# Attention values with P as the moving operand: one matmul per head for four half products

## The chip, the cores and the metric

One core of a Trainium2 chip runs the whole program. The metric is the device time of one execution in microseconds (us). The kernel before took 1598.1 us as the median of 3 runs (1597.1 to 1598.14).

## The reference

Two layers with residuals on x of shape (32, 128, 1024), all in float32. The first mixes the 128 rows of each batch by a matrix gathered with that batch's index; the second is causal attention with 16 heads of 64 columns.

```python
w = weights[conditions]                       # 200 matrices of 128x128
x = x + einsum('bct,bcd->bdt', x, w)
q, k, v = (heads(einsum('bsd,ed->bse', x, W)) for W in (Wq, Wk, Wv))
q = q * minimum(cond, 4.0)
scores = einsum('bhqd,bhkd->bhqk', q, k) / sqrt(64)
attn = softmax(where(causal, scores, min), axis=-1)
out = einsum('bhqk,bhkd->bhqd', attn, v)
x = x + einsum('bsd,ed->bse', rejoined(out), Wo)
```

## The kernel before

The stages are: an opening (first layer for batch 0, lines 384 to 394, and the first blocks of V from line 646); the rest of the first layer with V for the other batches; the attention stage, from step T_ATT to T_END; the output products of four batches; and fourteen pairs of batches of output products at the end. V, the halves of X, attention rows and prepared weights go through scratch in HBM.

The attention stage has 16 groups (8 groups of four batches, twice for half of the heads) of four cells, 64 cells. A cell n is one pair of heads for four batches and has 16 steps: eight for the q block, eight for the k block, both in TensorE's banks PJ. The scores, masks, exponentials, norms, turns and values of the cell are placed in the steps of the next one, at a step a that lies five after its k block:

- `pe_scores` (line 726): per batch one product of 256 columns, the two heads beside each other; the other head's rows of K are zero.
- DVE masks and takes the row maximum (lines 1126, 1132), ACT exponentiates with the row sum (957), DVE takes the reciprocal (1136), POOL multiplies (1239). P stands in PP with queries in the partitions.
- `dve_turn` (line 1011): ten transposes of 32 partitions per cell, five at a + 8 and five at a + 13, put the blocks on and below the diagonal at their turned place in PT.
- ACT makes PTH from PT (line 962, at a + 14), POOL makes PTL (1243).
- `pe_values` (line 737): per batch three matmuls of 256 columns, at a + 18 and a + 20; V's chunk of 128 columns (both heads) is stationary and the turned P of both heads moves. Half of what comes out pairs a head with the other head's P and is dropped.
- ACT copies the rows that are used to AT (lines 970, 971), and SP stores them (1538).

V of a group comes in two transfers (line 1400); ACT and POOL split it (921, 1233) into VH and VL. X of the next group comes in eight pieces, six steps apart (line 1388). Beside this, in a step of 48 of the cells that is otherwise quiet, a piece of Wq, Wk (16 of them) or Wo (32) is split by ACT and DVE (934 and 1107, 986 and 1150) and stored. Wq and Wk of the second half of the heads are loaded during the eighth and ninth group (line 1364), and Wo from 34 steps ahead of T_END.

Of the kernel before, what the change touches and what calls it, by code (L numbers as in the profile page):

```python
# [45 lines left out]
def cond_attention(nc, x, idx, cond, w0, wq, wk, wv, wo, mask_d, ident_d, out):  # L46
# [14 lines left out]
    with ExitStack() as ctx:  # L61
# [46 lines left out]
        with nc.sbuf_tensor("t_Y1", [128, DC, 256], f32) as tile:  # L108
            Y1 = tile
        VH = [sb("VH0", [128, GB, 512], f32r)]  # L110
# [7 lines left out]
        with ExitStack() as early:  # L118
            BH = sb("BH", [128, 4, 512], f32r, early)
            BL = sb("BL", [128, 4, 512], f32r, early)  # L120
        VH.append(sb("VH1", [128, GB, 512], f32r))
# [23 lines left out]
        WEH = sb("WEH", [128, 4, 512], f32r)  # L145
        WEL = sb("WEL", [128, 4, 512], f32r)
# [9 lines left out]
        QL = sb("QL", [128, T], f32r)  # L156
        PTH = sb("PTH", [128, GB, 256], f32r)
        PTL = sb("PTL", [128, GB, 256], f32r)
        AT = sb("AT", [128, 2, 2, 2, 128])
# [7 lines left out]
        PV = [pb("PV0"), pb("PV1")]  # L167
# [23 lines left out]
        act_pt, pool_pt, act_at = sem("pt_high"), sem("pt_low"), sem("at_out")  # L191
# [9 lines left out]
        l_y = [sem(f"load_y{n}") for n in range(2)]  # L201
# [4 lines left out]
        s_at = [[sem(f"store_at{n}_{k}") for k in range(2)] for n in range(2)]  # L206
# [13 lines left out]
        mask_at, exp_at, recip_at, norm_at, turn0_at, turn1_at, half_at, ptl_at, at_at = (At() for _ in range(9))  # L220
# [124 lines left out]
        for j in range(NGRP):  # L345
            t0 = T_ATT + STEPS * j
            for c in range(NC):
# [1254 lines left out]
```

## Time and profile before

| | us |
|---|---|
| median of 3 runs | 1598.1 |
| profiled execution | 1599.05 |
| its span, first to last instruction | 1597.7 |
| TensorE busy | 1587.2 (99%) |
| VectorE busy | 1016.6 (64%) |
| ScalarE busy | 820.4 (51%) |
| GpSimd busy | 739.2 (46%) |

The profile is of one execution; its own time is the span and 1.35 us around it. PE is TensorE's matmuls and PEld its weight loads, which overlap them. Busy times of one engine's groups overlap as well where its instructions are pipelined, so the distance from one matmul's start to the next one's says more than its duration.

### The profile page before, as it was taken

The numbers are of one execution on the slowest core, as the hardware profiler recorded it, in microseconds if no ns is written. First come the engines' busy times: TensorE is split into PE (matmuls) and PEld (weight loads), VectorE is DVE, ScalarE is ACT, GpSimd is POOL, SyncE is SP. The second block draws the span as 40 slices with busy tenths as digits, with TensorE's granted clock in tenths as the row PEclk, the third lists the DMA queues.
The fourth block names the chain that finished last, engine by engine and source line by source line (L and its number), as shares of the span: only waits on it lengthen the run. The fifth ranks groups of instructions, "written<-read, shape, count | busy, mean of one in ns | idle before, by whom it ended". The sixth has DMA issues, their size and how long they took to land.

```text
span 1597.7 us, 23102 instructions
## 1 busy us (share of the span) xinstructions
PE 1587.2 (99%) x7810; PEld 1338.5 (84%) x7810; DVE 1016.6 (64%) x2008; ACT 820.4 (51%) x2221; POOL 739.2 (46%) x618
## 2 busy tenths in 40 slices
PE   8999999999999999999999999999999999999999
PEld 7888888888888888888888888888888888888887
DVE  5844544543577777777776777777777755555553
ACT  6645545542466666665666666566666632222220
POOL 1545555552344434434544553454455334555552
PEclk9999999999999999999999999999999999999999
DMA  9857888866954465455529654553542596444442
GB/s 325 326 219 273 311 289 283 291 235 211 315 179 160 146 206 169 165 139 177 164 85 299 197 153 139 176 152 132 161 158 80 204 333 254 174 168 165 165 158 86
DMA packets 162086, 320.43 MB, mean 201 GB/s; under 512 B 13746, under 2 KB 81586, under 8 KB 155826
## 3 DMA queue, kind: packets, MB, share of 16 engines
q1 hardware_dynamic: 161970, 318.97, 59.1%
q8 instruction: 62, 1.02, 0.3%
q14 instruction: 54, 0.44, 0.1%
HBM read 184.70 MB, written 134.22 MB: 200 GB/s over the span
## 4 chain that ended last, share of the span: by engine, by line
PE 93%; DVE 2%; SPq 2%; DMA 1%; POOL 0%; issue 0%; ACT 0%; ACTq 0%; POOLq 0%
PE p_PJ L642 21%; PE p_PJ L643 21%; PE p_PJ L644 20%; PE p_SC L644 6%; PE p_SC L643 6%; PE p_SC L642 6%; PE p_PV L642 3%; PE p_PV L644 3%; PE p_PV L643 3%; PE p_LP L642 1%; PE p_LP L644 1%; PE p_LP L643 1%; SPq L1364 1%; PE p_PV L774 1%; PE p_LP L774 1%; DVE t_WSL L1103 1%
## 5 line engine op out<-in xcount | busy, mean ns | idle before, releaser
L643 PE MATMUL p_PJ<-t_XL,t_WH 128*128 128x512 f32 x1008 | 394.7, 392 | 0.0
L642 PE MATMUL p_PJ<-t_XH,t_WH 128*128 128x512 f32 x1008 | 394.6, 391 | 0.0
L644 PE MATMUL p_PJ<-t_XH,t_WL 128*128 128x512 f32 x1008 | 392.1, 389 | 0.0
L1243 POOL TENSOR_TENSOR t_PTL<-t_PT,t_PTH 128x512 fp32r<-128x512 f32 x128 | 163.0, 1294 | 382.5 <-ACT t_PTH L962 382.5
L1021 DVE STREAM_TRANSPOSE t_PT<-t_PP 32x256 f32<-32x256 f32 x640 | 278.2, 435 | 10.9 <-POOL t_PP L1239 1.2
L957 ACT ACTIVATE t_PP<-t_PP,t_st 128x128 f32<-128x128 f32 x512 | 198.5, 390 | 50.1 <-DVE t_st L1132 50.0
L644 PEld LDWEIGHTS p_PJ<-t_XH,t_WL 128*128 128x128 f32 x1008 | 189.3, 188 | 40.6
L642 PEld LDWEIGHTS p_PJ<-t_XH,t_WH 128*128 128x128 f32 x1008 | 189.8, 188 | 31.1
L643 PEld LDWEIGHTS p_PJ<-t_XL,t_WH 128*128 128x128 f32 x1008 | 190.2, 189 | 29.9
L962 ACT ACTIVATE t_PTH<-t_PT 128x512 fp32r<-128x512 f32 x128 | 73.8, 624 | 194.7 <-DVE t_PT L1021 194.7
L1239 POOL TENSOR_TENSOR t_PP<-t_PP,t_st 128x512 f32<-128x512 f32 x128 | 132.7, 1043 | 55.0 <-DVE t_st L1136 55.0
L1126 DVE SCALAR_TENSOR_TENSOR t_PP<-p_SC,t_beta,t_mask 128x256 f32<-128x256 f32 x256 | 111.5, 477 | 45.1 <-PE p_SC L644 45.1
L1113 DVE TENSOR_TENSOR t_KL<-p_PJ,t_KH 64x512 fp32r<-64x512 f32 x128 | 88.2, 689 | 53.4 <-ACT t_KH L944 51.3
L1233 POOL TENSOR_TENSOR t_VL<-t_VX,t_VH 128x512 fp32r<-128x512 f32 x64 | 92.0, 1458 | 65.0 <-ACT t_VH L921 65.0
L944 ACT ACTIVATE t_KH<-p_PJ 64x512 fp32r<-64x512 f32 x128 | 75.8, 592 | 87.2 <-PE p_PJ L644 85.6
L1228 POOL TENSOR_TENSOR t_xl<-t_XT,t_xh 128x512 fp32r<-128x512 f32 x56 | 74.4, 1328 | 95.0 <-ACT t_xh L844 94.3
L957 ACT ACTIVATION_READ_ACCUMULATOR t_PP<-t_PP,t_st 128x1 f32 x512 | 95.9, 187 | 0.0
L1132 DVE TENSOR_REDUCE t_st<-t_PP 128x2 f32<-128x256 f32 x256 | 94.1, 409 | 0.0
L1136 DVE RECIPROCAL t_st<-t_st 128x4 f32<-128x4 f32 x128 | 22.8, 178 | 87.2 <-ACT t_PP L957 87.2
L1087 DVE TENSOR_TENSOR t_SL<-t_SUM,t_SH 128x512 fp32r<-128x512 f32 x42 | 32.4, 772 | 69.6 <-ACT t_SH L875 69.6
L642 PE MATMUL p_PV<-t_PTH,t_VH 128*128 128x256 f32 x256 | 72.0, 281 | 1.6 <-POOL t_PTL L1243 1.6
L644 PE MATMUL p_PV<-t_PTH,t_VL 128*128 128x256 f32 x256 | 72.3, 282 | 0.0
(248 smaller groups left out, 3602.9 us busy)
## 6 DMA issues: line engine op xcount, KB each, us to landing
t_XH<-xth_scratch SPq DMA_DIRECT2D x56, 512.0 KB, 6.4
t_XL<-xtl_scratch SPq DMA_DIRECT2D x56, 512.0 KB, 6.6
v_scratch<-t_VR SPq DMA_DIRECT2D x64, 256.0 KB, 4.2
xth_scratch<-t_XH SPq DMA_DIRECT2D x16, 1024.0 KB, 3.9
xtl_scratch<-t_XL SPq DMA_DIRECT2D x16, 1024.0 KB, 6.3
t_VX<-v_scratch SPq DMA_DIRECT2D x32, 512.0 KB, 4.9
at_scratch<-t_AT SPq DMA_DIRECT2D x128, 128.0 KB, 1.8
t_XT<-x SPq DMA_DIRECT2D x31, 512.0 KB, 4.7
```

Of the source, the lines that this page charges most:

```text
L642: pe.matmul(bank, lh, rh, start=first, stop=False, skip_group_check=goes_on)
L643: pe.matmul(bank, lh, rl, start=False, stop=False, skip_group_check=goes_on)
L644: return pe.matmul(bank, ll, rh, start=False, stop=last, skip_group_check=goes_on)
L944: act.activation(KH[r, :, 128 * h:128 * h + 128], pj[r], ACT.Copy).then_inc(act_k, 1)
L957: act.activation(PP[:, u, h, :], PP[:, u, h, :], ACT.Exp, bias=st[:, 0, u, h:h + 1], scale=1.0, accum_out=st[:, 1, u, h:h + 1]).then_inc(a ...
L1021: m = dve.transpose(pt[32 * j:32 * j + 32, :, 32 * i:32 * i + 32], pp[32 * i:32 * i + 32, :, 32 * j:32 * j + 32])
L1113: dve.tensor_tensor(KL[r, :, k], pj[r], KH[r, :, k].bitcast(f32), ALU.subtract).then_inc(dve_k, 1)
L1126: dve.scalar_tensor_tensor(out=PP[:, u], in0=SC[u // 2][:, 256 * (u % 2):256 * (u % 2) + 256].rearrange("p (h k) -> p h k", h=2), scalar=b ...
L1132: dve.tensor_reduce(st[:, 0, u, :], PP[:, u], AX, ALU.max, negate=True).then_inc(dve_m, 1)
L1233: pool.tensor_tensor(VL[j % 2][:, u, :], VX[:, u, :], VH[j % 2][:, u, :].bitcast(f32), ALU.subtract).then_inc(pool_vl, 1)
L1239: pool.tensor_tensor(pp, pp, r, ALU.mult).then_inc(pool_n, 1)
L1243: pool.tensor_tensor(PTL[:, u:u + 2], PT[:, u:u + 2], PTH[:, u:u + 2].bitcast(f32), ALU.subtract).then_inc(pool_pt, 1)
```

## The change

Values. V is stored as VV, per batch and head a block of 128 columns that holds the high and the low half of that head's 64 columns side by side (for the second head of a pair in the other order). P is stored as PS, per batch and head 256 columns, the high half and then the low half. One matmul per head has the first as its stationary and the second as its moving operand. It gives four products in one bank half: V high x P high and V high x P low in 64 partitions, V low x P high and V low x P low in the other 64.

```diff
-            to = PV[k][:, z * 256:z * 256 + 256]
-            three(to, VH[j % 2][:, u, cc], VL[j % 2][:, u, cc], PTH[:, u, :], PTL[:, u, :], True, True).then_inc(pe_pv, 1)
+            for h in range(2):
+                moving = PS[:, 2 * u + h].rearrange("p a q -> p (a q)")
+                mm = pe.matmul(PV2[:, z, 256 * h:256 * h + 256], VV[j % 2][:, u, 2 * c + h, :], moving, start=True, stop=True)
+            mm.then_inc(pe_pv, 1)
```

Both banks now hold one pair of batches, and the values of a pair wait until DVE has summed the pair before (`dve_M`). ACT copies V low x P high across to the partitions that it belongs to (AC), DVE adds the two products of V high in PSUM by a reduction, and POOL adds the two.

```diff
-                    act.activation(dst[0:64], pv[0:64, :, 0, :], ACT.Copy).then_inc(act_at, 1)
-                    act.activation(dst[64:128], pv[64:128, :, 1, :], ACT.Copy).then_inc(act_at, 1)
+                    act.activation(AC[0:64, k], PV2[64:128, :, 0:128], ACT.Copy).then_inc(act_c, 1)
+                    act.activation(AC[64:128, k], PV2[0:64, :, 256:384], ACT.Copy).then_inc(act_c, 1)
...
+                    for h in range(2):
+                        r = slice(64 * h, 64 * h + 64)
+                        both = PV2[r, :, 256 * h:256 * h + 256].rearrange("p u (a q) -> p u q a", a=2)
+                        dve.tensor_reduce(AT[r, k], both, AX, ALU.add).then_inc(dve_M, 1)
...
+                    pool.tensor_tensor(AT[:, P % 2], AT[:, P % 2], AC[:, P % 2], ALU.add).then_inc(pool_at, 1)
```

Turning. DVE transposes 32x32 blocks of all 128 partitions at once, two batches per instruction, into TB; ten transfers of 32 partitions with 1 KB each take the blocks on and below the diagonal to their rows, in one of two tiles by turns. The turn of the next cell waits for these transfers, and so does ACT's high half of P, which stands in ACT's order ahead of the high half of K.

```diff
-            for i, j in tri[5 * part:5 * part + 5]:
-                m = dve.transpose(pt[32 * j:32 * j + 32, :, 32 * i:32 * i + 32], pp[32 * i:32 * i + 32, :, 32 * j:32 * j + 32])
+            pp = PP[:, 2 * k:2 * k + 2].rearrange("p u h (j c) -> p j (u h) c", j=4)
+            dve.transpose(turned(n)[:, :, 4 * k:4 * k + 4, :], pp).then_inc(dve_t, 1)
...
+            for i in range(4):
+                for j in range(i + 1):
+                    src = turned(n)[32 * i:32 * i + 32, j].rearrange("a u q -> a (u q)")
+                    sp.dma_start(p_tile(n)[32 * j:32 * j + 32, i, :], src).then_inc(l_P, 16)
```

The order of a cell, of the loads of X and of the loads of V:

```diff
-                turn0_at.put(a + 8, n)
-                turn1_at.put(a + 13, n)
+                move_at.put(a + 10, n)
...
-                    half_at.put(a + 14 + k, P)
-                    ptl_at.put(a + 15 + 2 * k, P)
-                    v = a + 17 + k if n == 4 * NGRP - 1 else a + 18 + 2 * k
+                    turn_at.put(a + 7.5 + 1.5 * k, P)
+                    last = n == 4 * NGRP - 1
+                    half_at.put(a + (20 if last else 25.25) + 0.5 * k, P)
+                    ptl_at.put(a + (20.75 if last else 26) + 1.5 * k, P)
+                    v = a + (25.25 + 3.25 * k if last else 29 + 4.5 * k)
+                    own = v + (1.75 if n >= 4 * NGRP - 2 else (1.75, 8.5)[k])
...
-                    at_at.put(v + (0.75 if n == 4 * NGRP - 1 else 5.25), P)
+                    other_at.put(v + 0.75, P)
+                    own_at.put(own, P)
+                    at_at.put(own + 1.25, P)
...
-                    X_load.put(t0 - STEPS + (12 + 5 * i if j == 1 else 24 + 4 * i if j == NG + 1 else 1 + 6 * i), (j, i))
+                    X_load.put(t0 - STEPS + (12 + 5 * i if j == 1 else 24 + 4 * i if j == NG + 1 else (1, 6, 17, 22, 33, 38, 49, 54)[i]), (j, i))
...
-                V_load.put(t0 + (-11, 2.75)[k] if j == 0 else t0 - STEPS + (28 if j == 1 else 0.25), (j, k))
+                V_load.put(t0 + (-11, 2.75)[k] if j == 0 else t0 - STEPS + (28 if j == 1 else 10), (j, k))
```

Opening. ACT's fourth weight copy and the second batch's weight copy come later, and TensorE gets nine matmuls of zeros.

```diff
-            w_high.put((-8.5, -7.75, -6, -5, -0.5, 0.5, 1.5, 2.5)[d], d)
-            w_low.put((-7.5, -6.5, -5, -4, 0.5, 1.5, 2.5, 3.5)[d], d)
+            w_high.put((-8.5, -7.75, -6, -2.75, -0.5, 0.5, 1.5, 2.5)[d], d)
+            w_low.put((-7.5, -6.5, -5, -2, 0.5, 1.5, 2.5, 3.5)[d], d)
...
-            l0_wh.put(p - 1, bb)
-            l0_wl.put(p - 0.5, bb)
+            l0_wh.put(p - (0.5 if bb == 1 else 1), bb)
+            l0_wl.put(p - (0.25 if bb == 1 else 0.5), bb)
...
                     pe_l0_a(bb, h)
+                    if bb == 0 and h == 1:
+                        pe_zeros(3)
...
                     pe_l0_b(bb, h)
+                    if bb == 0 and h == 1:
+                        pe_zeros(6)
```

For room, the rows of the output stage use one buffer where they had two, and some tiles of the last cells lie elsewhere.

## Rows read from the trace of the kernel before

**Rows 1.** The page: busy us per engine; the chain that ended last, by engine

```profile
PE 1587.2 (99%) x7810; PEld 1338.5 (84%) x7810; DVE 1016.6 (64%) x2008; ACT 820.4 (51%) x2221; POOL 739.2 (46%) x618
...
PE 93%; DVE 2%; SPq 2%; DMA 1%; POOL 0%; issue 0%; ACT 0%; ACTq 0%; POOLq 0%
```

**Rows 2.** Busy us by stretch, granted clock, DMA share, GB/s

```profile
0.00:20.00 20.00, 15.53 (x62) 11.91 (x63) 10.55 (x19) 12.85 (x23) 3.11 (x10) 1.00 0.84 298
...
480.00:900.00 420.00, 418.91 (x2189) 359.67 (x2188) 314.77 (x726) 261.92 (x819) 194.30 (x160) 1.00 0.55 173
```

**Rows 3.** Waits of PE from 450 to 1360 us: total, times, longest

```profile
PE p_PV L642 <- POOL t_PTL L1243: 1.6, 2, 1.1
```

**Rows 4.** Groups of PE: shapes and count, busy us, mean ns, idle before

```profile
L643 PE MATMUL p_PV<-t_PTL,t_VH 128*128 128x256 f32 x256 | 72.2, 282 | 0.0
```

**Rows 5.** Timeline of PE and its weight loads, one cell: start, us

```profile
701.36 0.28 PE L642 MATMUL p_SC<-t_KH,t_QH 128*128 128x256 f32 x1
...
704.18 0.28 PE L642 MATMUL p_PV<-t_PTH,t_VH 128*128 128x256 f32 x1
704.18 0.19 PEld L643 LDWEIGHTS p_PV<-t_PTL,t_VH 128*128 128x128 f32 x1
...
704.89 0.40 PE L642 MATMUL p_PJ<-t_XH,t_WH 128*128 128x512 f32 x1
...
715.18 0.28 PE L642 MATMUL p_SC<-t_KH,t_QH 128*128 128x256 f32 x1
```

**Rows 6.** Groups of DVE, ACT and POOL from 480 to 1360 us

```profile
L1021 DVE STREAM_TRANSPOSE t_PT<-t_PP 32x256 f32<-32x256 f32 x592 | 257.4, 435 | 10.3 <-POOL t_PP L1239 1.2
...
L1132 DVE TENSOR_REDUCE t_st<-t_PP 128x2 f32<-128x256 f32 x236 | 86.7, 409 | 0.0
...
L971 ACT ACTIVATE t_AT<-p_PV 64x256 f32<-64x256 f32 x120 | 45.5, 379 | 2.9
...
L1243 POOL TENSOR_TENSOR t_PTL<-t_PT,t_PTH 128x512 fp32r<-128x512 f32 x120 | 152.8, 1294 | 362.5 <-ACT t_PTH L962 362.5
```

**Rows 7.** Timeline of DVE in the same cell

```profile
707.43 0.69 DVE L1116 TENSOR_TENSOR t_QL<-p_PJ,t_QH 128x512 fp32r<-128x512 f32 x1 [0.45 <-ACT t_QH L952]
...
710.38 1.07 DVE L1150 TENSOR_TENSOR t_OL<-t_xr,t_OH 128x512 fp32r<-128x512 f32 x1
711.92 1.41 DVE L1113 TENSOR_TENSOR t_KL<-p_PJ,t_KH 64x512 fp32r<-64x512 f32 x2 [0.48 <-ACT t_KH L944]
```

**Rows 8.** Timeline of ACT and POOL in the same cell

```profile
706.59 0.19 ACT L957 ACTIVATION_READ_ACCUMULATOR t_PP<-t_PP,t_st 128x1 f32 x1
706.80 0.60 ACT L952 ACTIVATE t_QH<-p_PJ 128x512 fp32r<-128x512 f32 x1
...
707.07 1.04 POOL L1239 TENSOR_TENSOR t_PP<-t_PP,t_st 128x512 f32<-128x512 f32 x1 [0.50 <-DVE t_st L1136]
```

**Rows 9.** Timeline of SP's queue: stores of attention rows

```profile
721.91 1.13 SPq L1538 DMA_DIRECT2D at_scratch<-t_AT  x2
```

**Rows 10.** The view of line 1538, the stores of attention rows

```profile
DMA to landing us min/median/max: 1.7/1.8/10.9
```

**Rows 11.** The view of line 1364, the loads of Wq and Wk

```profile
DMA to landing us min/median/max: 4.4/8.1/13.1
```

**Rows 12.** The page's DMA issues: KB each, median us to landing

```profile
t_XH<-xth_scratch SPq DMA_DIRECT2D x56, 512.0 KB, 6.4
```

**Rows 13.** Timeline of PE and ACT in the opening

```profile
11.03 0.66 PE L774 MATMUL p_LP<-t_ident,t_XT 128*128 128x128 f32 x4 [0.53 <-ACT t_XT L900]
11.53 0.65 PE L774 MATMUL p_PV<-t_ident,t_XT 128*128 128x128 f32 x4
13.79 0.47 PE L642 MATMUL p_PJ<-t_WSH,t_XH 128*128 128x512 f32 x1 [1.61 <-DVE t_XL L1035]
...
12.13 0.31 ACT L895 ACTIVATE t_wh<-t_wr 128x128 fp32r<-128x128 f32 x1 [0.66 <-POOL t_wr L1220]
12.34 0.58 ACT L856 ACTIVATE t_XH<-p_LP 128x512 fp32r<-128x512 f32 x1
```

More of the change, by code:

```diff
@@ L109, in cond_attention @@
             Y1 = tile
+        with nc.sbuf_tensor("t_VV0", [128, GB, 8, 128], f32r) as tile:
+            VV = [tile]
         VH = [sb("VH0", [128, GB, 512], f32r)]
@@ L120, in cond_attention @@
             BL = sb("BL", [128, 4, 512], f32r, early)
+        with nc.sbuf_tensor("t_VV1", [128, GB, 8, 128], f32r) as tile:
+            VV.append(tile)
         VH.append(sb("VH1", [128, GB, 512], f32r))
@@ L145, in cond_attention @@
         WEH = sb("WEH", [128, 4, 512], f32r)
+        with nc.sbuf_tensor("t_TB", [128, 4, 8, 32], f32) as tile:
+            TB = tile
+            with nc.sbuf_tensor("t_PT2", [128, GB, 256], f32) as tile:
+                PT2 = tile
         WEL = sb("WEL", [128, 4, 512], f32r)
@@ L200, in cond_attention @@
         l_V = [sem(f"load_v{n}") for n in range(2)]
-        l_y = [sem(f"load_y{n}") for n in range(2)]
+        l_y = sem("load_y")
         l_x1 = [sem(f"load_x1_{n}") for n in range(4)]
@@ L205, in cond_attention @@
         s_V = [sem(f"store_v{n}") for n in range(4)]
-        s_at = [[sem(f"store_at{n}_{k}") for k in range(2)] for n in range(2)]
+        s_at = [sem(f"store_at{k}") for k in range(2)]
         s_out = [sem(f"store_out{n}") for n in range(4)]
@@ L566, in operand, with turned, p_tile, v_high @@
             return tuple(four(h) for h in halves)
+        def turned(n):
+            return TB[:] if n < 58 else WR[:].rearrange("p a (b c) -> p (a b) c", b=2).rearrange("p j (u q) -> p j u q", u=8)
+        def p_tile(n):
+            return PT if n % 2 == 0 else PT2 if n < 58 else xr[1][:].rearrange("p (i q) -> p i q", i=4)
+        def v_high(tile, u):
+            return tile[:, u].rearrange("p (a b) (c e) -> p a (b c) e", b=2, c=2)[:, :, 0:4:3, :]
+        def v_low(tile, u):
+            return tile[:, u].rearrange("p (a b) (c e) -> p a (b c) e", b=2, c=2)[:, :, 1:3, :]
+        def by_heads(rows):
+            return rows.rearrange("p (a b e) -> p a b e", a=4, b=2)
+        def p_half(P, low):
+            u = 4 * (P % 2)
+            return PS[:, u:u + 4, low, :].rearrange("p u (i q) -> p u i q", i=4)
+        def p_raw(P):
+            u = 4 * (P % 2)
+            return p_tile(P // 2)[:].rearrange("p i (u q) -> p u i q", u=8)[:, u:u + 4]
         def w_sum(i):
@@ L599, in out_tile @@
         def out_tile(o):
[L600 removed]
+            return LATE[:, o % 4, :] if o % 4 >= 2 else xr[0][:, 512 * (o % 2):512 * (o % 2) + 512]
         def wo_rows(place):
@@ L1257, in pool_program @@
                             pool.wait_ge(s_O, 32 * 32)
-                            for n in range(2):
-                                for k in range(2):
-                                    pool.wait_ge(s_at[n][k], 16 * 32)
+                            for k in range(2):
+                                pool.wait_ge(s_at[k], 16 * 64)
                         pool.tensor_tensor(sums(0), a21, a22, ALU.add).then_inc(pool_S, 1)
@@ L1412, in sp_wait_at, with sp_move_p @@
         def sp_wait_at(rounds):
-            for n in range(2):
-                for k in range(2):
-                    sp.wait_ge(s_at[n][k], 16 * (NC // 2) * rounds)
+            for k in range(2):
+                sp.wait_ge(s_at[k], 16 * NC * rounds)
+        def sp_move_p(n):
+            sp.wait_ge(dve_t, 2 * n + 2)
+            if n == 0:
+                sp.wait_ge(pool_z, 5)
+            elif n >= 2:
+                sp.wait_ge(pool_pt, 2 * n - 2)
+            if n == 59:
+                sp.wait_ge(pool_z, 6)
+            for i in range(4):
+                for j in range(i + 1):
+                    src = turned(n)[32 * i:32 * i + 32, j].rearrange("a u q -> a (u q)")
+                    sp.dma_start(p_tile(n)[32 * j:32 * j + 32, i, :], src).then_inc(l_P, 16)
         def sp_load_y(y):
@@ L1532, in sp_program @@
                     sp_load_W(n, part)
+                for n in move_at(tick):
+                    sp_move_p(n)
                 for P in at_at(tick):
```

111 lines of the change are left out of this document (62 added, 49 removed).

## The prediction

> **What bounds the kernel now.** Read first the page's busy times and the chain that ended last [rows 1]: TensorE is busy 1587.2 us of a span of 1597.7 us, and PE holds 93% of the chain, VectorE 2%. No other engine passes 64%. The stretches say the same of the attention stage alone [rows 2]: from 480 to 900 us PE is busy 418.91 of 420 us, while DVE has 314.77, ACT 261.92 and POOL 194.30; from 0 to 20 us PE lacks 4.5 us. The waits of PE between 450 and 1360 us are one line, 1.6 us in all [rows 3]. So in the attention stage time is the number of matmuls times their pitch, and whatever takes matmuls away shortens the span as long as nothing else becomes late.
>
> A matmul's busy time is not its pitch, because they overlap: the value product is three groups of 256 matmuls, one shown, with 282 ns each [rows 4]. The pitch is read off the timeline [rows 5]: the six value matmuls of two batches run from 704.18 to the next projection matmul at 704.89, 0.71 us, so 0.118 us each. One cell (the q and k blocks of a head pair, four batches of scores, four of values) lasts from the scores at 701.36 to the next scores at 715.18, 13.82 us; there are 64 cells.
>
> **What the change removes from PE.** Per batch and head pair there were three matmuls of 256 columns and there are now two: 768 become 512. 256 x 0.118 = 30.3 us. Per cell that is 0.47 us, so the cell falls to 13.35 us. Operands keep 128 columns of weights and 256 moving ones, so I take the same pitch.
>
> **DVE.** Out go ten transposes of 32x256 per cell, at 0.435 us [rows 6]: 4.35 us. In come two of 128x512 and four reductions of 64x512. Neither stands in the trace. For the transpose the bounds are 0.44 us (partitions cost nothing and neither do columns) and 0.87 (twice the 256-column one); I take 0.70: the 512-column subtraction of the low half of Q [rows 7] has 0.69 on the same engine, nearer to it in size than the narrow transpose. For the reduction: 0.41 (the 128x256 one) [rows 6] and 0.82; I take 0.68. Sum 2 x 0.70 + 4 x 0.68 = 4.1 us, so DVE's load stays. Its order does not: the whole turning and one pair of reductions now stand ahead of the low half of K, where only half of the transposes stood.
>
> That order is a loop from scores to next scores. In the cell shown, counted from the scores at 701.36: the last exponential is read out at 706.78 and POOL's norm ends at 708.11 [rows 8], 6.75 us on. ACT now has two copies of 0.379 us [rows 6] between the exponentials, so 7.5 us. DVE then does the low half of Q (7.5), two turns (8.9), two reductions (10.3), the low half of a weight piece, 1.07 us (11.4), and the low half of K, 1.41 us [rows 7] (12.8). The next scores come at 13.35, and they wait for that last one. Slack 0.6 us; at both upper prices none (2 x 0.17 + 2 x 0.14 = 0.62); so nothing in the sum, but it is thin in the 48 cells that split a weight piece (16 of Wq and Wk, 32 of Wo). Elsewhere it is 1.6 us.
>
> **ACT and POOL.** ACT's copies per cell stay four of 64x256, its high half of P stays two of 128x512. POOL gains two additions of 128x256 per cell, between 0.5 us (half the norm) [rows 8] and 1.3 (the subtraction) [rows 6]; I take 0.6. With 194 of 420 us busy this is hidden; without that cover it would be 1.2 us per cell. The three-dimensional strides of P and V change no element count; I take the same durations.
>
> **The wait for a single pair of banks.** Values of one pair of batches now need the sum of the pair before it. From the first to the second pair in a cell lie 4.5 steps of 0.69 us (13.82 less four blocks of 0.71, over 16), two blocks of scores of 0.71 and the matmuls themselves, 5.0 us; the way over ACT (0.76), DVE (1.36) and handovers needs 3.2. No cost.
>
> **The transfers.** Ten of 32 KB per cell go through SP between two waits. SP issues one in 0.32 to 0.56 us (two of the stores of attention rows take 1.13) [rows 9], so ten take 3.2 to 5.6 us of a 13.35 us cell. Those stores land in 1.8 us as a median, 10.9 at most [rows 10]. Ends: 5 us when the queue is empty, 16.5 when it is full. They have from 8.9 us after one cell's scores, when the turn ends, to ACT's high half in the next, which stands behind the high half of Q at 706.80 [rows 8], delayed by 0.75 to the copy's end: 20.1 us. So 11.2 us of room for 5 to 7 us. Queued behind SP's wait for the turn are the stores of weight pieces and of attention rows and the next loads of X; behind ACT's wait for the transfers stand the high half of K and so the scores.
>
> Two places are tight. Where Wq and Wk of the second half are loaded, landings have a median of 8.1 us and go to 13.1 [rows 11]: ten transfers behind them arrive up to 16.5 - 11.2 = 5 us late, in two or three cells; I take 3 us in all, bounds 0 to 12. And the last piece of X is issued 10 steps ahead of its group instead of 21: 7.3 us against a landing of 6.4 [rows 12]; late by up to 1 us in 12 groups, so 0 to 12, and I take 1, because pieces are now spaced apart. The end (Wo loaded beside the last cells) I leave at 0, bounds 0 to 4: outputs that follow have 16 steps of room.
>
> Of these small transfers the Trainium skill says ("DMA: Bandwidth & Descriptors", Anatomy of one DMA, and Bandwidth) that each DMA has a fixed part of about 2.0 us and that below 64 KB descriptors dominate. It measured this on the GpSimd path; the two stores were issued within 1.13 us here and land in 1.8 each, so the fixed parts overlap. If they did not, ten would need an estimated 20 us.
>
> **The opening.** V's first block starts at 13.79 us [rows 13]. ACT's copy of X waits until 12.34, behind a weight copy that waits for a transfer, although the transposes were issued by 11.53. The new order puts X ahead. But the 3 + 6 zero matmuls of 0.23 us fill 2.1 us that were idle (0.53 and 1.61), and PE takes them in order: the six run from about 12.0 to 13.4. Gain 0.4 us, bounds -0.5 (they delay) and 1.2 (all of the copy's delay). The clock gains nothing: granted 1.00 over 0 to 20 us already [rows 2].
>
> **Sum**, against the profiled execution of 1599.05 us (span 1597.7 and 1.35 around it; 0.95 above the median of 1598.1): 1599.05 - 30.3 - 0.4 + 3 + 1 = 1572.4, and on the scale of the median 1571.4. Forecast 1571 us. From no change this kernel can be told at about 0.2%, 3.2 us.
>
> **The rivals.**
> - *The saving is kept, less a few us of late transfers* (the forecast), 1564 to 1578: for it stand the single PE wait and the slacks of 0.6, 1.8 and 5 us above. Chance 0.62.
> - *DVE's loop binds.* If turn and reductions come at their upper prices and ACT's copies wait 0.3 us for values amid the exponentials, the cell is the loop. 0.3 us x 48 cells = 14 us; X late in 12 groups gives as much. 1577 to 1592. For it: slack that reaches nothing; against: my middle prices. Chance 0.21.
> - *All is given back*, 0.47 us per cell on average, 1595 to 1601. Chance 0.04.
> - *The transfers bind, slower than before.* The turn of the next cell and ACT's high half both wait for the ten. The point is 11.2 + 0.47 = 11.7 us from turn to last landing; at 12.7 us the kernel takes 1598 + 64 = 1662. For it: landings of up to 10.9 us in this queue [rows 10]; against: the median of 1.8 and the DMA share of 0.55 in the stage [rows 2]. Chance 0.10. By the fixed part that the Trainium skill gives (same page), taken one after another, it would be an estimated 20 us per cell and over 2100.
> - *PE does not get faster*: weight loads take 0.19 us each [rows 5], and if the turned products ran at that, 512 x 0.19 = 97 against 91 us, 1604. Against: the same loads run today at a pitch of 0.118. Chance 0.03.
>
> So faster 0.83, same 0.04, slower 0.13. The range, 1564 to 1592, takes in the forecast's own bounds and the second rival; above it 0.17 is left out, and nearly nothing below, since 1598.1 - 30.3 - 1.2 is 1566.6.
>
> **What would show it.** The value product: 512 matmuls at 0.118 us pitch, scores to scores 13.35 us in a cell. PE's waits in the attention stage: a few us, on POOL's low half of P around the weight loads; much time under the low half of K would be the second rival, and ACT's high half of P waiting in every cell for a transfer the fourth. Turn near 0.7, reduction near 0.68 us, last landing 5 to 7 us after the turn. V's first block near 13.4 us. I am wrong if PE waits over 10 us in that stage.

## The result: slower by 3%, and the profile after

The changed kernel takes 1646.53 us (median of 4 runs, 1644.19 to 1651.84), the kernel before beside it 1598.12: a ratio of 1.0305, 95% interval 1.0292 to 1.0318. Forecast were 1571 us and a range of 1564 to 1592. The profiled execution took 1646.84 us, its span is 1645.5.

First the page's busy times, the chain that ended last, and, among the DMA issues, one group of X's loads and the transfers, as in [rows 1, 12]:

```profile
PE 1582.5 (96%) x7563; PEld 1323.8 (80%) x7563; DVE 987.1 (60%) x1752; ACT 817.6 (50%) x2221; POOL 850.2 (52%) x748
...
PE 74%; DMA 8%; SPq 8%; issue 3%; ACT 3%; POOL 2%; DVE 2%; ACTq 0%; DVEq 0%; POOLq 0%
...
t_XL<-xtl_scratch SPq DMA_DIRECT2D x56, 512.0 KB, 5.7
t_PT<-t_TB SPq DMA_DIRECT2D x580, 32.0 KB, 1.9
```

Two sums differ from before. PE's idle time was 10.5 us (1597.7 - 1587.2) and is 63.0: 52.5 more. PE's busy time should have fallen by the 30.3 us of the matmuls taken out, to 1556.9, and fell by 4.7: 25.6 came back. 52.5 + 25.6 - 30.3 = 47.8 us, the difference of the spans.

The idle time is in PE's waits (in us: total, times, longest), where [rows 3] had 1.6 us in one line:

```profile
PE p_PJ L690 <- DMA t_XL<-xtl_scratch: 34.4, 12, 5.8
PE p_PV L797 <- POOL t_PS L1308: 10.5, 3, 6.0
PE p_PV L797 <- DVE t_AT L1199: 8.2, 4, 4.7
PE p_PJ L690 <- DVE t_KL L1164: 2.6, 1, 2.6
```

Twelve waits are for the last piece of X, one at the start of a group. The others stand where Wq, Wk and Wo are loaded, and at the end.

The busy time that came back is mostly the clock. The mean granted clock is 0.984 after and 1.000 before; at 2.4 or 1.2 GHz that makes 0.016 x 1645.5 / 0.5 = 53 us at the lower one. The stretches, with PE's busy time first, then the other engines, and near the end the granted clock, the DMA share and GB/s (compare [rows 2]); the third holds one of the twelve waits and the stretch at half clock around its end:

```profile
0.00:20.00 20.00, 18.11 (x74) 14.39 (x75) 10.47 (x18) 12.94 (x23) 3.35 (x10) 1.00 0.87 300
480.00:900.00 420.00, 399.80 (x2000) 339.04 (x2000) 288.74 (x585) 251.57 (x792) 232.71 (x210) 0.98 0.65 191
672.60:679.40 6.80, 4.15 (x10) 3.30 (x11) 0.04 (x1) 0.00 (x0) 0.62 (x1) 0.50 0.57 155
```

The timeline of PE in that place, the two scores that bound the cell behind it, and four value matmuls of a later cell with the matmul behind them:

```profile
675.25 0.76 PE L690 MATMUL p_PJ<-t_XH,t_WH 128*128 128x512 f32 x1 [5.20 <-DMA t_XL<-xtl_scratch]
675.82 0.63 PE L691 MATMUL p_PJ<-t_XL,t_WH 128*128 128x512 f32 x1
676.24 0.63 PE L692 MATMUL p_PJ<-t_XH,t_WL 128*128 128x512 f32 x1
...
680.50 0.39 PE L690 MATMUL p_PJ<-t_XH,t_WH 128*128 128x512 f32 x1
680.73 0.39 PE L691 MATMUL p_PJ<-t_XL,t_WH 128*128 128x512 f32 x1
...
681.86 0.28 PE L690 MATMUL p_SC<-t_KH,t_QH 128*128 128x256 f32 x1
...
695.19 0.28 PE L690 MATMUL p_SC<-t_KH,t_QH 128*128 128x256 f32 x1
...
733.48 0.63 PE L797 MATMUL p_PV<-t_PS,t_VV 128*128 128x256 f32 x4
733.95 0.40 PE L690 MATMUL p_PJ<-t_XH,t_WH 128*128 128x512 f32 x1
```

PE waits 5.20 us, and then the matmuls start 0.42 us apart; from 679.4 on, when the clock is back, they start 0.23 apart. At half clock a us is worth 0.23 / 0.42, so 0.45 us of it is lost; 53 us cost 24 us if PE works all the time, and less as part of it is still the wait (2.65 of the 6.80 us above). So about 20 of the 25.6 us: added up from the starts of the matmuls, the twelve stretches at half clock inside the trace lose 1.3 to 2.5 us each, 20.0 together. Another 2.6 are the zero matmuls of the opening, which make PE busy where it was idle (18.11 of the first 20 us against 15.53 in [rows 2]). The last 3 I have not settled. The Trainium skill says ("TensorE: Matmul & The Clock Gate", HAM oscillation — how this bites in real kernels) that work which waits for its loads starts each new tile at the throttled clock. The trace agrees for eight of the twelve waits: the granted clock falls between 2.7 us before and 1.2 us after their ends. At the other four, of 0.57, 0.91, 1.49 and 2.03 us, it does not fall, nor anywhere in this stage of the kernel before, with 1.6 us of waits in all.

Away from the group's start the cell is what was promised: 681.86 to 695.19 is 13.33 us, 13.82 before [rows 5]. So the saving is made in the cells, and more than lost at their seams. The new parts among the page's groups (busy us, mean ns, idle before), to compare with [rows 4, 6]:

```profile
L1199 DVE TENSOR_REDUCE t_AT<-p_PV 64x256 f32<-64x512 f32 x256 | 174.0, 680 | 78.9 <-ACT t_AC L1025 59.1
...
L1311 POOL TENSOR_TENSOR t_AT<-t_AT,t_AC 128x256 f32<-128x256 f32 x128 | 122.0, 953 | 129.4 <-DVE t_AT L1199 129.4
...
L797 PE MATMUL p_PV<-t_PS,t_VV 128*128 128x256 f32 x512 | 84.8, 289 | 18.6 <-POOL t_PS L1308 10.5
```

And the turn among DVE's groups from 480 to 1360 us, which also shows that it seldom waits for the transfers of the cell before:

```profile
L1074 DVE STREAM_TRANSPOSE t_TB<-t_PP 128x512 f32<-128x512 f32 x106 | 68.7, 686 | 8.8 <-DMA t_PT<-t_TB 8.8
```

Why X is late shows in the timeline of SP's queue ahead of a group's start, compare [rows 9]. SPq marks the time in which SP issues a transfer:

```profile
717.32 6.21 SPq L1498 DMA_DIRECT2D t_PT<-t_TB  x10
723.57 0.58 SPq L1523 DMA_DIRECT2D woh_scratch<-t_OH  x1
724.20 0.44 SPq L1525 DMA_DIRECT2D wol_scratch<-t_OL  x1
724.68 0.45 SPq L1622 DMA_DIRECT2D at_scratch<-t_AT  x1
725.17 0.45 SPq L1455 DMA_DIRECT2D t_XH<-xth_scratch  x1
725.67 0.46 SPq L1622 DMA_DIRECT2D at_scratch<-t_AT  x1
726.17 0.43 SPq L1455 DMA_DIRECT2D t_XL<-xtl_scratch  x1
```

The ten transfers hold SP for 6.2 us (0.63 each), five stores and loads follow, and the last piece of X is asked for at 726.17. Its slot, ten steps of 13.33 / 16 = 0.83 us ahead of the group's start at 730.75, was 722.4: it is issued 3.8 us late, 1.1 of them until the ten are out and 2.6 behind the five that had queued up. It lands in 5.0 us, and PE waits 0.57 us. This is the mildest of the twelve; reckoned in the same way the others are issued 3.8 to 7.9 us late and land in 5.3 to 7.8 us.

### The profile page after: what moved, and what is told of

It reads as the page before. It is cut to its first block, busy times and chain, and to the rows that moved or that the text cites. A ratio compares the mean times of both kernels' runs of the same rounds, so it can differ in the third digit from the quotient of the medians.

```text
span 1645.5 us, 23425 instructions
## 1 busy us (share of the span) xinstructions
PE 1582.5 (96%) x7563; PEld 1323.8 (80%) x7563; DVE 987.1 (60%) x1752; ACT 817.6 (50%) x2221; POOL 850.2 (52%) x748
## 4 chain that ended last, share of the span: by engine, by line
PE 74%; DMA 8%; SPq 8%; issue 3%; ACT 3%; POOL 2%; DVE 2%; ACTq 0%; DVEq 0%; POOLq 0%
PE p_PJ L690 16%; PE p_PJ L691 16%; PE p_PJ L692 16%; PE p_SC L692 5%; PE p_SC L690 5%; PE p_SC L691 5%; DMA t_XL<-xtl_scratch 4%; SPq L1498 4%; PE p_PV L797 3%; ACT t_PP L1010 1%; PE p_PV L690 1%; POOL t_VV L1299 1%; PE p_PV L692 1%; PE p_PV L691 1%; PE p_LP L690 1%
## 5 line engine op out<-in xcount | busy, mean ns | idle before, releaser
L690 PE MATMUL p_PJ<-t_XH,t_WH 128*128 128x512 f32 x1008 | 402.2, 399 | 37.1 <-DMA t_XL<-xtl_scratch 34.4
L691 PE MATMUL p_PJ<-t_XL,t_WH 128*128 128x512 f32 x1008 | 400.6, 397 | 0.0
L692 PE MATMUL p_PJ<-t_XH,t_WL 128*128 128x512 f32 x1008 | 398.4, 395 | 0.0
L1199 DVE TENSOR_REDUCE t_AT<-p_PV 64x256 f32<-64x512 f32 x256 | 174.0, 680 | 78.9 <-ACT t_AC L1025 59.1
L1311 POOL TENSOR_TENSOR t_AT<-t_AT,t_AC 128x256 f32<-128x256 f32 x128 | 122.0, 953 | 129.4 <-DVE t_AT L1199 129.4
L1308 POOL TENSOR_TENSOR t_PS<-t_PT,t_PS 128x512 fp32r<-128x512 f32 x122 | 157.7, 1293 | 19.4 <-ACT t_PS L1017 19.4
L1024 ACT ACTIVATE t_AC<-p_PV 64x256 f32<-64x256 f32 x128 | 48.8, 381 | 146.3 <-PE p_PV L797 144.8
L1299 POOL TENSOR_TENSOR t_VV<-t_VX,t_VV 128x512 fp32r<-128x512 f32 x64 | 81.4, 1292 | 75.0 <-ACT t_VV L974 75.0
L797 PE MATMUL p_PV<-t_PS,t_VV 128*128 128x256 f32 x512 | 84.8, 289 | 18.6 <-POOL t_PS L1308 10.5
L797 PEld LDWEIGHTS p_PV<-t_PS,t_VV 128*128 128x128 f32 x512 | 76.5, 196 | 26.8 <-POOL t_PS L1308 18.9
```

The costliest lines, as they stand in the source:

```text
L690: pe.matmul(bank, lh, rh, start=first, stop=False, skip_group_check=goes_on)
L691: pe.matmul(bank, lh, rl, start=False, stop=False, skip_group_check=goes_on)
L692: return pe.matmul(bank, ll, rh, start=False, stop=last, skip_group_check=goes_on)
L797: mm = pe.matmul(PV2[:, z, 256 * h:256 * h + 256], VV[j % 2][:, u, 2 * c + h, :], moving, start=True, stop=True)
L1199: dve.tensor_reduce(AT[r, k], both, AX, ALU.add).then_inc(dve_M, 1)
L1299: pool.tensor_tensor(v_low(VV[j % 2], u), by_heads(VX[:, u, :]), v_high(VV[j % 2], u).bitcast(f32), ALU.subtract).then_inc(pool_vl, 1)
```

## The experiments

Theory A: transfers are late because of what stands ahead of them in SP's queue and in the DMA engines, X most of all, and each long wait of PE then costs half clock as well. Rivals: bytes (the DMA engines are full), VectorE's loop, or the opening. All diffs but the first are excerpts.

### X earlier, and X from another queue

Only the slots of X's pieces go back to those of the kernel before:

```diff
-else (1, 6, 17, 22, 33, 38, 49, 54)[i]), (j, i))
+else 1 + 6 * i), (j, i))
```

> The changed kernel with the loads of X back at every sixth step (1 + 6i) from the start of the group before, so the eighth piece is issued at step 43 and not 54. Theory A (ten issues of 0.63 us occupy SP for 6.3 us per cell, and the last pieces of X stand behind them): PE's wait for X falls from 34.4 us to under 3, the half-clock stretches that follow these waits go too (10 of 13, about 35 us at half clock, so 17 us), and the time falls from 1646.5 to about 1595 us (1588 to 1602). Theory B (the transfer engines are full and pieces land late wherever they are issued): X's wait stays over 10 us, or turns into a wait for P of the same size, and the time stays over 1615.

1605.3 us (median of 5), ratio to the kernel before 1.0041 (1.0026 to 1.0055). Of the waits, this is left:

```profile
PE p_PV L797 <- POOL t_PS L1308: 11.3, 3, 6.1
PE p_PV L797 <- DVE t_AT L1199: 9.7, 4, 4.2
PE p_PJ L690 <- DMA t_XL<-xtl_scratch: 4.0, 1, 4.0
```

The slots of X alone were worth 41 us, of which 30 are PE's idle time and the rest its busy time, with the clock (0.984 to 0.990). Theory B, over 1615, is excluded; A's 1602 is missed by 3 us, as the other waits stayed. From 480 to 780 us PE has 300.00 of 300 us busy, with all ten transfers per cell in place.

Second, the slots stay late, but ACT issues X's pieces:

```diff
+                for j, i in X_load(tick):
+                    sp_load_X(j, i)
                 for n in kh_ev(tick):
...
-        def sp_load_X(j, i):
+        def sp_load_X(j, i, sp=act):
...
-                for j, i in X_load(tick):
-                    sp_load_X(j, i)
```

> The changed kernel with its own slots for X, but issued from ScalarE's queue, ahead of the high half of K. Theory A (SP's order): the wait for X falls under 6 us without any other slot; ACT pays about 0.9 us per cell for two issues, part of it ahead of K's high half; 1592 to 1615 us. Theory B (full transfer engines): X's wait stays over 20 us and the time over 1630.

1605.14 us (one run), and no wait for X is left at all, at the same slots and with the same bytes. So it was the place in SP's queue and not the DMA engines. It was not free: the ten transfers now land in 3.3 us as a median instead of 1.9, and PE waits 13.7 us for DVE's row sums (8.2 before) and 4.4 us for a load of weights at 425. The Trainium skill says ("DMA: Bandwidth & Descriptors", Issuing engines are not separate DMA queues) that a second issuing engine saves only the sequencer's time, usually small beside the transfer. The first half the run bears out: X's high and low halves land in 4.4 and 5.2 us as medians, against 5.0 and 5.7 from SP, so nearly all that was saved is time in SP's queue. The second half does not hold for the ten transfers: from the first issue to the last landing they take 8.1 us, and 6.2 of these are issue.

### The opening alone

The kernel before with the other opening:

```diff
-            w_high.put((-8.5, -7.75, -6, -5, -0.5, 0.5, 1.5, 2.5)[d], d)
+            w_high.put((-8.5, -7.75, -6, -2.75, -0.5, 0.5, 1.5, 2.5)[d], d)
...
+                        pe_zeros(3)
...
+                        pe_zeros(6)
```

> The kernel before with the other opening alone (two weight copies later, nine matmuls of zeros). Theory A (the first block of V starts 0.4 us earlier, as in the changed kernel: 13.40 against 13.79): 1597.7 us, 0.2 to 0.6 us under 1598.1, which no run tells from no change at 0.2%. Rival (the zeros keep the clock up or delay later work): over 1 us to either side, with a wait of PE behind 20 us that the kernel before does not have.

1597.52 us (median of 10), ratio 0.9993 (0.9983 to 1.0003): no difference that can be told. V's first block starts at 13.02 us there and at 13.40 in the changed kernel, 13.79 before [rows 13].

### Half of the transfers

Five of the ten transfers per cell are left out, and with them the turned blocks of the last 32 queries and one more; the values are computed from zeros there.

```diff
-                for j in range(i + 1):
+                for j in range(max(0, i - 1), i + 1) if i < 3 else ():
```

> The changed kernel with five of the ten transfers of P per cell left out, so that half of P's blocks are zero in the products; all else stands. Theory A (SP's time per issue): SP is free 3.2 us earlier in each cell, more than the mean wait for X of 2.9 us; the wait falls under 8 us, the half-clock stretches behind it go, and the time is 1595 to 1610 us. Theory B (full transfer engines): 10 MB of 341 less change little, X's wait stays over 20 us and the time over 1625.

1583.1 us (one run), below even A's 1595 to 1610, and B's 1625 is excluded. X's slots stand where they do in the changed kernel, and its waits fall from 34.4 us to 2.6; the clock is 0.998:

```profile
PE p_PV L797 <- POOL t_PS L1308: 4.5, 2, 3.5
PE p_PV L797 <- DVE t_AT L1199: 2.7, 2, 2.3
PE p_SC L690 <- DVE t_XL L1213: 2.6, 1, 2.6
PE p_PJ L690 <- DMA t_XL<-xtl_scratch: 2.6, 4, 1.1
```

3.1 us of SP per cell were worth 63 us of the whole, and 15 of the 30 us of the matmuls show once SP has time.

### Without transfers: the old turning

The new value product with the ten narrow transposes of before, straight into the rows:

```diff
-            dve.transpose(turned(n)[:, :, 4 * k:4 * k + 4, :], pp).then_inc(dve_t, 1)
+            for i, j in [(i, j) for i in range(4) for j in range(i + 1)][5 * k:5 * k + 5]:
+                to = p_tile(n)[32 * j:32 * j + 32, i, :].rearrange("p (u q) -> p u q", u=8)
+                m = dve.transpose(to, pp[32 * i:32 * i + 32, :, 32 * j:32 * j + 32])
+            m.then_inc(dve_t, 1)
...
-                for n in move_at(tick):
-                    sp_move_p(n)
```

> The changed kernel as it is, but P turned as before, by ten narrow transposes on VectorE straight into its rows (five behind the norm, five later), without transfers; the new value product, its reductions and sums stay. VectorE: 314.8 us in 420 before is 10.4 us per cell, and four reductions of 0.68 make 13.1 of a cell of 13.35 us. Theory A (the transfers cost what the change lost; VectorE alone has just not the room for both): no wait for X, but waits of PE for VectorE's low halves and row sums in most cells, 13.5 to 13.9 us per cell, 1580 to 1610. Rival D (VectorE has the room after all and the transfers were not needed): 1566 to 1576. Rival E (VectorE's order binds hard, and the clock falls behind each wait): over 1620.

1745.97 us (median of 2), ratio 1.0925 (1.0903 to 1.0947): over 1620, as in rival E, though not by the clock, and my 13.5 to 13.9 us per cell were wrong. The waits of PE, one kind in 116 places:

```profile
PE p_PV L797 <- DVE t_AT L1203: 142.2, 116, 1.6
```

One cell of DVE's timeline, from the reciprocals to the next cell's scores:

```profile
701.72 0.18 DVE L1191 RECIPROCAL t_st<-t_st 128x4 f32<-128x4 f32 x1 [0.90 <-ACT t_PP L1010]
703.26 0.18 DVE L1191 RECIPROCAL t_st<-t_st 128x4 f32<-128x4 f32 x1 [1.37 <-ACT t_PP L1010]
703.74 0.69 DVE L1171 TENSOR_TENSOR t_QL<-p_PJ,t_QH 128x512 fp32r<-128x512 f32 x1 [0.30 <-ACT t_QH L1005]
704.60 2.23 DVE L1077 STREAM_TRANSPOSE t_PT<-t_PP 32x256 f32<-32x256 f32 x5 [0.16 <-POOL t_PP L1309]
706.86 1.41 DVE L1203 TENSOR_REDUCE t_AT<-p_PV 64x256 f32<-64x512 f32 x2
708.30 1.41 DVE L1168 TENSOR_TENSOR t_KL<-p_PJ,t_KH 64x512 fp32r<-64x512 f32 x2
709.63 2.24 DVE L1077 STREAM_TRANSPOSE t_PT<-t_PP 32x256 f32<-32x256 f32 x5
711.89 1.41 DVE L1203 TENSOR_REDUCE t_AT<-p_PV 64x256 f32<-64x512 f32 x2
713.34 0.88 DVE L1181 SCALAR_TENSOR_TENSOR t_PP<-p_SC,t_beta,t_mask 128x256 f32<-128x256 f32 x2
```

From one cell's masks (L1181) to the next one's DVE works but for 0.90, 1.37, 0.30 and 0.16 us, in which it waits for ACT and POOL; from 704.60 on it has no pause at all. 13.1 us of work, as the expectation adds it up, and 2.7 of such waits are 15.8; the cells take 16.2 (PE waits for row sums at 692.21 and again at 708.41). I had added up loads where a loop decides. So with this value product, and in this order of operations, DVE has no room for the old turning, and the transfers, or another relief of DVE, are needed. Other orders were not tried.

### Drawing the loads apart

With X early, the waits left stand where large loads are asked for between a turn and its transfers. The next kernels keep X early and move only slots and, where named, the issuing engine.

Loads of the second half's Wq and Wk spread out (excerpt; an item is weight, part, high or low):

```diff
-        for d, item in ((57, (2, 1)), (57.25, (2, 2)), (64.5, (3, 1)), (70, (3, 2)), (100, (2, 0)), (104, (3, 0))):
+        for d, item in ((23.5, (2, 1, 0)), (27, (2, 1, 1)), (39.5, (3, 1, 0)), (43, (3, 1, 1)), (57, (2, 2, 0)), (71.5, (2, 2, 1)),
+                        (75, (3, 2, 0)), (87.5, (3, 2, 1)), (103.5, (2, 0, 0)), (104.5, (2, 0, 1)), (106.5, (3, 0, 0)), (107.5, (3, 0, 1))):
```

> The changed kernel with X's pieces early (1605.3 us) and, besides, the loads of Wq and Wk for the second half drawn apart: the first columns' successors are asked for 33 steps earlier, and high and low halves stand in separate gaps between two bursts of ten transfers; the first group's X pieces stand in such gaps too. Theory A (a transfer is late because of what stands ahead of it on SP and in the DMA engines, and PE's wait then also costs half clock): the waits at 438, 793, 845, 862 and 894 us (14.3 us together) go, and the 20 us at half clock behind them (10 us lost): 1580 to 1590. Rival B (in that stretch the bytes to be moved are too many, whatever their order): the same bytes, so 1600 to 1606.

1598.5 us (median of 10), ratio 1.0003 (0.9994 to 1.0013). The waits at 845 and 862 us are gone; those at 439 and 794 stayed, and the last piece of X at 889 waits 6.2 us, behind the loads of the first 128 columns of Wq and Wk that I had put ahead of it and ten transfers. 6.8 us are gained over X early alone, where 15 to 25 were expected, and neither A's range nor B's has the result.

The end's fetches of Wo in gaps too:

```diff
-        for k, t in ((1, T_END - 22), (3, T_END - 34), (0, T_END - 7), (2, T_END + 2),
-                     (6, T_END + 11), (5, T_END + 19), (4, T_END + 31), (7, T_END + 43)):
+        for k, t in ((1, T_END - 24), (3, T_END - 9), (0, T_END + 3), (2, T_END + 23),
+                     (6, T_END + 32), (5, T_END + 38), (4, T_END + 44), (7, T_END + 50)):
```

> As the kernel with the weights drawn apart, and the fetches of Wo's halves at the end drawn apart too: none stands between the turn of one of the last three cells and its ten transfers. Theory A: the waits at 1261, 1291 and 1307 us (10.7 us) go, with 10 us at half clock behind them (5 us lost): 13 to 16 us under the kernel with the weights drawn apart alone, about 1566 to 1577. Rival C (the end is bound by the chain from the last exponentials to the last values, not by transfers): no more than 3 us less.

1601.71 us (median of 8), 1.0023 (1.0012 to 1.0033): a miss. The wait at 1255 went, but at 1293 PE still waits 5.1 us for POOL's low half, although the last transfer was issued at 1286.59 and had landed by 1288.5, and a fetch put later now makes PE wait 4.3 us itself. The time is as rival C had it, but its chain is not what holds POOL there:

```profile
1287.85 0.43 SPq L1622 DMA_DIRECT2D at_scratch<-t_AT  x1
...
1289.98 1.41 DVE L1201 TENSOR_REDUCE t_AT<-p_PV 64x256 f32<-64x512 f32 x2 [5.61 <-DMA at_scratch<-t_AT]
...
1291.47 0.72 POOL L1313 TENSOR_TENSOR t_AT<-t_AT,t_AC 128x256 f32<-128x256 f32 x1 [8.68 <-DVE t_AT L1201]
1292.15 2.48 POOL L1310 TENSOR_TENSOR t_PS<-t_xr,t_PS 128x512 fp32r<-128x512 f32 x2
```

A store of attention rows is issued behind the ten transfers. DVE's next row sums wait 5.61 us for it, POOL's addition waits 8.68 us for these, and the low half of P stands behind that addition in POOL's order. So this too is a transfer behind others, one that I had not listed.

The stores of attention rows from ACT's queue:

```diff
-                    sp.wait_ge(pool_at, P + 1)
-                    sp.dma_start(at_d[GROUP[j]][:, t0:t0 + 256], AT[:, k].rearrange("p u s -> p (u s)")).then_inc(s_at[k], 16)
...
+                    act.wait_ge(pool_at, P + 1)
+                    act.dma_start(at_d[GROUP[j]][:, t0:t0 + 256], AT[:, k].rearrange("p u s -> p (u s)")).then_inc(s_at[k], 16)
```

> As the kernel with weights and end drawn apart, and the two stores of attention rows per cell issued by ScalarE's queue instead of SP's. Theory A in its strong form (SP's 0.45 us per store, and its wait for the sum of the rows, still hold up transfers): waits of PE for the value product's sums fall, 3 to 8 us less. Rival (with the loads apart SP has room, and ScalarE now waits for GpSimd's sum instead): within 3 us, or up to 5 us more with waits of PE for exponentials or for the high half of K.

1627.62 us (median of 4), 1.0183 (1.0166 to 1.0200). ACT now waits 93.4 us, at 45 places, for POOL's sum amid its exponentials, and PE 30 times for the row sums, 30.3 us in all. Neither the theory nor the rival had this: a wait moved onto an engine with a loop costs in cell after cell.

All at once, with W's first columns in two gaps, V of the second group later, and the last cell's values five to six steps later:

```diff
-        W1_load.put(t + 3, 0)
+        for i, d in enumerate((8, 23.5, 25.5, 28)):
+            W1_load.put(t + d, i)
...
-                    v = a + (25.25 + 3.25 * k if last else 29 + 4.5 * k)
+                    v = a + (30 + 3.25 * k if last else 29 + 4.5 * k)
```

> The changed kernel with X early, and with all large loads of the attention stage put between the bursts of ten transfers: the four loads of first columns in two gaps instead of one, the second half's Wq and Wk over three cells more, X of the groups with two sources of load earlier, V of the second group later; at the end Wo's fetches in gaps, and the last cell's values, with what follows from them, 5 to 6 steps later. In the kernel with the weights alone drawn apart (span 1597.8) PE still waits 3.4, 2.3, 6.2, 2.4, 1.8 and 4.3 us and runs 34 us at half clock. Theory A (lateness of transfers is what is left, and it is a matter of order): at least 12 of these 20 us go, and half of the time at half clock: 1570 to 1585, so under the kernel before by 0.8% or more. Rival B (bytes, not order): some of the waits move elsewhere, 1592 to 1602.

1592.97 us (median of 10), 0.9968 (0.9959 to 0.9978): under the kernel before by 0.3%, but 8 us over the most that A expected, and in rival B's range. PE waits 5.9 us for row sums, as the store that DVE's next sum waits for lands behind weights, 4.2 at 1261, where ACT waits for y (attention rows read back for the output products) ahead of its high half, and 5.7 at 1317 and 1327.

That store between two of the ten transfers:

```diff
                     sp.dma_start(p_tile(n)[32 * j:32 * j + 32, i, :], src).then_inc(l_P, 16)
+                    if (i, j) == (2, 1) and n >= 2:
+                        sp_store_at(2 * n - 3)
```

> The kernel with all large loads drawn apart (median 1593.0), and the store of attention rows that is ready when a burst of ten transfers begins stands after the sixth of them instead of behind the tenth and whatever follows; at the end the last load of y goes ahead of a fetch of Wo, and two fetches stand 4 to 8 steps later. Left in that kernel: waits of PE for row sums of 1.4, 2.7 and 1.6 us between 823 and 857 (VectorE waits 3.04 us for that store at 838.29), 4.2 at 1261 (ScalarE waits 4.44 us for y ahead of its high half of P), 3.9 and 1.8 at 1317 and 1327 (GpSimd waits 15.2 us for the last store), and 13.5 us at half clock. Theory A: these 15.6 us fall to under 5 and most of the half clock goes: 1572 to 1583. Rival (each shift only moves the wait to the next transfer in the queue): 1588 to 1595.

1594.49 us (median of 10), 0.9972 (0.9963 to 0.9981): no gain, as the rival had it. PE waits 4.8 us at 856 in place of three shorter ones. At the end the 4.2 us at 1261 went, but 1.2 to 1.7 us at 1246, 1275 and 1290 came, and 3.9 and 2.8 stand at 1318 and 1328.

Weights over one more gap, ACT's copy of y behind its high half of P, and the last four stores from ACT, which is nearly idle at the end:

```diff
+                for P in at_at(tick - 3 * TICK // 4):
+                    if P >= 124:
...
+                        act.wait_ge(pool_at, P + 1)
+                        act.dma_start(at_d[GROUP[NGRP - 1]][:, t0:t0 + 256], AT[:, k].rearrange("p u s -> p (u s)")).then_inc(s_at[k], 16)
```

> The kernel with all large loads drawn apart (median 1593.0; not the store between transfers), with three edits: the second half's Wq and Wk loads are spread over one more gap, so that no gap between bursts holds over 2.5 MB; ScalarE's copy of y at the end stands behind its high half of P instead of ahead of it; the last four stores of attention rows are issued by ScalarE, which is nearly idle then, and so stand behind no fetch of Wo in SP's queue. Left before: 5.6 us of waits for row sums between 823 and 857, 4.2 at 1261, 5.7 at 1317 and 1327, and 13.5 us at half clock. Theory A (each wait has its own transfer ahead of it, and goes when that is gone): at least 10 of these 15.5 us and half of the half clock go, 1576 to 1584. Rival (the two dense stretches, around the change of weights and at the end, have no order that fits, so waits only move, as the store between transfers did): 1589 to 1596.

1589.47 us (median of 5), 0.9945 (0.9931 to 0.9958), in the rival's range and not in A's. The last scores are now at 1256 us, but PE waits 5.8 us at 1288: the store before these four was still in SP's queue behind the last transfers, and ACT stood 11.5 us in its wait for POOL's sum, ahead of its high half of P.

Three more of them, and two fetches later:

```diff
-                    if P >= 124:
+                    if P >= 121:
```

> The kernel before this one (median 1589.5), with three more stores of attention rows at the end on ScalarE's queue (the last seven instead of the last four), two fetches of Wo 4 steps later, and one weight load of the dense stretch one gap later. There the store that VectorE's row sums of the last cell need was issued by SP behind the last ten transfers (at 1280.82), ScalarE stood 11.5 us in its wait for GpSimd's sum ahead of its high half of P, and PE waited 5.8 us at 1288, 2.0 at 1269, 3.1 at 1329 and 2.8 at 825, with 13.8 us at half clock. Theory A (each of these is one transfer behind others): the 5.8 and the 2.0 go, with 7 to 10 us at half clock behind them: 1576 to 1584. Rival (the end now is a chain of its own, from the last scores over turn, transfers, halves, rows and their sums, that no order of transfers shortens: 331 us from the last scores to the end, 315 in the kernel before): 1586 to 1592.

1586.04 us (median of 5), ratio 0.9920 (0.9906 to 0.9933): the fastest with all ten transfers, 60 us under the changed kernel and 13 under the one before. The 5.8 us at 1288 went; at 1269 PE still waits 2.5. Its waits of PE, the longest lines (at "issue" the profile shows nothing that PE waited for):

```profile
PE p_PV L805 <- DVE t_AT L1212: 6.5, 5, 2.5
PE p_SC L698 <- issue: 4.5, 1, 4.5
PE p_SC L698 <- DVE t_XL L1226: 2.5, 1, 2.5
```

And two stretches of it (PE's busy time first, the granted clock third from the end):

```profile
412.00:1240.00 828.00, 824.78 (x4203) 704.28 (x4202) 605.08 (x1221) 528.14 (x1655) 493.98 (x446) 1.00 0.65 195
1240.00:1350.00 110.00, 99.15 (x441) 80.36 (x440) 59.75 (x85) 31.13 (x79) 46.02 (x39) 0.97 0.78 279
```

From the first scores to the last this kernel takes 842.7 us (412.34 to 1255.07) and the one before 870.2 (412.75 to 1282.99): 27.5 of the 30.3 us are there. From the last scores to the end it takes 328.3 us against 314.7, so 13.6 are given back, in 10.9 us of waits between 1240 and 1350 and the clock's 0.97. That the end could be freed as well was not shown. The last three kernels all came out in their rivals' ranges and none in A's: that only order was wrong is shown for X, while for the change of weights and for the end it stays open whether any order would do. Each of these kernels also makes several edits at once, so no single one can be priced.

## Why the prediction was wrong

It was wrong in sign, and by its own criterion: PE waits 54 us between 450 and 1360 us, far over 10. Point by point:

- **The matmuls** (-30.3): right. Four of them take from 733.48 to 733.95, so 0.118 us each as forecast, scores to scores are 13.33 us (forecast 13.35), and 27.5 us are found in the best kernel.
- **DVE, ACT, POOL**: right in kind. The turn takes 0.69 us (0.70 taken), the reduction 0.68 (0.68). In the cell from 681.86 the low half of K ends 12.2 us after the scores, so 1.1 us of slack where I had 0.6. POOL's addition takes 0.95 us (0.6 taken, bounds 0.5 to 1.3), hidden as said. The second rival did not come true, though the old turning shows how near it lies.
- **The fourth rival**, slower because the ten transfers themselves come later than 11.7 us after the turn, is not what happened: they hold SP for 6.2 us and land 1.9 us after issue, 8.1 us in all. ACT waits for them at 5 places (21.2 us) and DVE at 4 (12.2 us), but what is issued behind them is late.
- **X's last piece: the step that failed.** The prediction put it as "issued 10 steps ahead of its group instead of 21: 7.3 us against a landing of 6.4 [rows 12]; late by up to 1 us in 12 groups", bounds 0 to 12, taken 1. The place and the count were right; the term measures 34.4 us and, with the clock, 41. Ten steps are 8.3 us by the cells as measured, so the 7.3 were not the trouble: I took the slot as the time of issue. But this slot falls behind ten transfers, and the sum for SP stood in the paragraph above: issue at 0.32 to 0.56 us each from [rows 9], so 3.2 to 5.6 us, was used for the transfers' own deadline only. It measures 6.2, the slot is 3.8 us late in the mildest group and 7.9 in the worst, and the landing comes on top.
- **The weights** (+3, bounds 0 to 12) **and the end** (0, bounds 0 to 4): right that these places are tight, but the terms were too small. With X early, they hold 21 us of waits for POOL's low half of P and for row sums. Not the transfers alone were late there: the store of attention rows made DVE's next row sums wait, as I had not listed. Their tile AT has one buffer for each half of a cell where it had two; what the second one would give back was not tried.
- **The clock**: I wrote "gains nothing", and meant that it is at full rate already. That it can be lost was no term. About 20 us, and it turns every long wait of PE dearer: in the one shown 5.2 us became 7.1, as 4.2 us of matmuls at 0.42 apart lost nearly 2.
- **The opening** (-0.4): the block moved as forecast to 13.40, but the time alone shows no difference.

With the terms as measured the sum is 1597.7 - 30.3 + 52.5 + 25.6 = 1645.5. It closes by construction, as the 25.6 were reckoned as what PE's busy time did not fall; found apart from it are 20.0 of clock and 2.6 of zeros.

## What to carry to other kernels

A queue that issues in order has a time budget of its own: multiply the transfers that a change adds by the issue time, and for everything scheduled behind them take the issue as late by that sum, before looking at landings. Most late loads were paid twice here, once as a wait of TensorE and once as half clock about its end, so a term for the clock belongs in the price of each long wait. And a wait should be moved to the engine that has nothing in a loop behind it: the same stores cost 26 us on ScalarE in every cell (1601.71 to 1627.62), and nothing that could be seen when, among other edits, the last seven went there, beside a ScalarE that is nearly idle.

## What the runs showed of the hardware that was not expected

A transfer of 32 KB between two places in SBUF, 32 partitions of 1 KB, holds SP for 0.63 us (ten in 6.21), where a store of 128 KB from 128 partitions or a load of 512 KB next to it takes 0.43 to 0.46. Issued from ACT, as in the second experiment, the same loads hold that queue for 0.33 us. So issue does not go by bytes, and with nothing queued up ten small transfers cost more of the queue than ten large ones; where loads crowd, one of 512 KB has held SP for up to 3.3 us. The landings of 1.9 us overlap: the last of ten lands about 1.9 us after its issue. The Trainium skill states a fixed part of about 2.0 us per DMA, measured on the GpSimd path ("DMA: Bandwidth & Descriptors", Anatomy of one DMA). The 1.9 agree with its size, and the rival that I had drawn from it, one after another, did not come true.

That the clock falls at all in a kernel whose PE is 96% busy, behind single gaps such as the one of 5.20 us, I had not expected; in the kernel with the old turning, 116 waits of at most 1.6 us each left it at 0.998.
